# Turning an expert's activations behind the first chunk of the next expert's product, and the turned gating columns in another bank

## What is computed

```python
# second layer: 8 experts, each token is sent to 2 of them
for e in range(E):
    h = jax.nn.gelu(xf @ we1[e] + be1[e], approximate=False)   # 512 -> 1024
    y = h @ we2[e] + be2[e]                                    # 1024 -> 512
    out = out + combine[:, e:e + 1] * y
# fourth layer, from a zero state, so that only three of the four gates count
gates = xt @ Wi + b
c = sigmoid(i_) * tanh(g_)
h = sigmoid(o_) * tanh(c);  y = h @ Wo + bo
```

## Time and profile before

| | us |
|---|---|
| three timed runs, median (lowest to highest) | 488.34 (482.66 to 490.34) |
| the profiled execution, its own time | 483.48 |
| its span, from the first to the last instruction | 481.7 |
| TensorE busy | 439.2 (91% of the span) |
| VectorE busy | 396.8 (82%) |
| ScalarE busy | 281.5 (58%) |
| feed-forward experts, steps 0 to 7 | from about 59 to 164 |
| LSTM experts, steps 0 to 7 | from about 329 to 436 |

### The profile page before, as it was taken

One profiled execution on the slowest core, in us unless ns is written; L12 is line 12 of the kernel. 1 busy time (PEld: TensorE's weight loads), 2 busy tenths in 40 slices (PEclk: granted clock), 3 DMA queues, 4 the chain that ended last, 5 costly groups with the idle time before them and its releaser, 6 DMA issues.

```text
span 481.7 us, 6148 instructions
## 1 busy us (share of the span) xinstructions
PE 439.2 (91%) x2214; PEld 351.2 (73%) x2214; DVE 396.8 (82%) x645; ACT 281.5 (58%) x306; POOL 106.6 (22%) x128
## 2 busy tenths in 40 slices
PE   3988799999999976899999998979899899999895
PEld 1655578788888766587899996647678788887674
DVE  8989868898889854687999979785898998978764
ACT  2245468768876744143444446254988788858631
POOL 5641000111100050146787300030001211000300
PEclk9999999999999997799999999988999999999897
DMA  7931557899998838378677333235688999975801
GB/s 256 304 124 44 190 199 270 303 353 358 377 361 320 340 105 366 105 267 312 190 208 260 97 109 140 103 135 174 246 306 322 348 373 363 363 299 215 353 2 45
DMA packets 25780, 115.67 MB, mean 240 GB/s; under 512 B 7036, under 2 KB 7708, under 8 KB 14864
## 3 DMA queue, kind: packets, MB, share of 16 engines
q1 hardware_dynamic: 18400, 93.90, 52.7%
q0 software_dynamic: 7056, 21.26, 13.4%
q10 hardware_dynamic: 288, 0.03, 0.1%
HBM read 108.63 MB, written 6.55 MB: 239 GB/s over the span
## 4 chain that ended last, share of the span: by engine, by line
PE 63%; DVE 21%; ACT 6%; DMA 5%; issue 3%; POOL 1%; DVEq 1%; ACTq 0%; SPq 0%; POOLq 0%
PE bank L1506 11%; PE bank L1507 11%; PE bank L1511 11%; DVE wlo L928 7%; PE bank L1499 4%; PE bank L1882 3%; PE bank L1500 3%; PE bank L1884 3%; PE bank L1501 3%; PE bank L1520 2%; DMA y_tok<-y_rows,row_i 2%; PE bank L1771 2%; PE bank L1709 2%; DMA raw<-in_weights_dram 1%; ACT whi L673 1%
## 5 line engine op out<-in xcount | busy, mean ns | idle before, releaser
L928 DVE TENSOR_TENSOR wlo<-raw,whi 128x2048 fp32r<-128x2048 f32 x73 | 165.2, 2287 | 15.0 <-ACT whi L673 14.5
L673 ACT ACTIVATE whi<-raw 128x2048 fp32r<-128x2048 f32 x73 | 137.6, 1914 | 8.3 <-PE bank L1851 6.4
L1506 PE MATMUL bank<-whi,xe_hi 128*128 128x512 f32 x192 | 77.2, 402 | 2.8 <-ACT xe_hi L702 1.4
L1507 PE MATMUL bank<-wlo,xe_hi 128*128 128x512 f32 x192 | 75.9, 395 | 0.0
L1511 PE MATMUL bank<-whi,xe_lo 128*128 128x512 f32 x192 | 52.4, 394 | 0.0
L1506 PE MATMUL bank<-whi,hT_hi 128*128 128x512 f32 (+1 forms) x124 | 49.8, 405 | 2.1 <-ACT hT_hi L730 1.4
L615 POOL DMA_INDIRECT xg<-node_rows,idx x12 | 14.4, 1202 | 156.9 <-DVE idx L1191 156.9
L1507 PE MATMUL bank<-wlo,hT_hi 128*128 128x512 f32 (+1 forms) x124 | 48.1, 391 | 0.0
L648 POOL DMA_INDIRECT gath<-node_rows,src_i x34 | 41.6, 1224 | 15.2 <-DVE mp L1423 8.7
L1506 PEld LDWEIGHTS bank<-whi,xe_hi 128*128 128x128 f32 x192 | 36.1, 188 | 11.6 <-issue 2.2
L1511 PEld LDWEIGHTS bank<-whi,xe_lo 128*128 128x128 f32 x192 | 36.1, 188 | 8.6
(11 more groups left out here) (307 smaller groups left out, 854.2 us busy)
## 6 DMA issues: line engine op xcount, KB each, us to landing
raw<-in_weights_dram SPq DMA_DIRECT2D x85, 1024.0 KB, 6.3
y_rows<-y_sb POOLq DMA_DIRECT2D x16, 256.0 KB, 5.9
ea<-in_ea_dram SPq DMA_DIRECT2D x8, 256.0 KB
node_rows<-xn POOLq DMA_DIRECT2D x4, 256.0 KB, 2.5
gath<-node_rows,src_i POOLq DMA_INDIRECT x34
x<-in_x_dram SPq DMA_DIRECT2D x1, 512.0 KB, 3.8
gw<-in_L_ffn_gw_dram SPq DMA_DIRECT2D x1, 512.0 KB, 10.2
node_rows<-A_sb POOLq DMA_DIRECT2D x2, 256.0 KB, 4.4
```

The costliest lines, as they stand in the source:

```text
L673: act.activation(whi[n % SPL][:, :, :], raw[n % RAW][:, :, :], ACT.Copy).then_inc(hi_cut, 1)
L928: dve.tensor_tensor(wlo[n % SPL][:, :, :], raw[n % RAW][:, :, :], whi[n % SPL][:, :, :].bitcast(f32), ALU.subtract).then_inc(lo_cut, 1)
L1506: pe.matmul(ps, xh[:, blocks + k, :], whi[w % SPL][:, k, cs], start=first and k == 0, stop=False)
L1507: pe.matmul(ps, xh[:, blocks + k, :], wlo[w % SPL][:, k, cs], start=False, stop=False)
```

## The change

On TensorE `turn_h(e - 1)` moves from the end of step e - 1 into `first_product(e)`, behind its first chunk. That first chunk now waits for only the first of the two counts of `h_ok` (`2e - 1`), since the bank that it writes has been read by then. Only the last expert's activations are turned at the end of a step, as before. The gating columns of `turn_g` go to bank 0 instead of bank 5, so `turn_g` no longer waits for `hT_lo`, nor `turn_h` for `idx_ok`; `turn_g` waits for the `idx` before its own. `biases`, which writes bank 0 later, waits for the last `idx`. The runs for experts with more than 128 tokens keep their order. On ScalarE and VectorE the cuts of a step move ahead of `turned`.

```diff
@@ ScalarE, experts
                     if step >= 2:
                         outputs(step - 2)
+                    if step >= 2:
+                        cuts(run.last_out(step - 2) + SPL + 1)
                     if step >= 1:
                         turned(step - 1)
...
-                    if step >= 2:
-                        cuts(run.last_out(step - 2) + SPL + 1)
                     results(step)
@@ VectorE, slots and experts
-                        dve.tensor_scalar(idx[:, e:e + 1], B[5][:, at:at + 1], -1.0, 0.0, ALU.add, ALU.max)\
+                        dve.tensor_scalar(idx[:, e:e + 1], B[0][:, at:at + 1], -1.0, 0.0, ALU.add, ALU.max)\
...
+                    if step >= 2:
+                        cuts(run.last_out(step - 2) + SPL + 1)
                     if step >= 1:
                         turned(step - 1)
-                    if step >= 2:
-                        cuts(run.last_out(step - 2) + SPL + 1)
                     results(step)
@@ TensorE, biases
+                pe.wait_ge(idx_ok, (E - 1) * nth - 1)
@@ TensorE, turn_g
-                    if e >= 3:
+                    if 2 < e <= E:
                         pe.wait_ge(*run.slot_read(e - 1))
-                    if e >= 3:
-                        pe.wait_ge(run.hT_lo, run.banks_h * (e - 2 if e < E else e - 1))
+                    if e >= E:
+                        pe.wait_ge(run.hT_lo, run.banks_h * (e - 1))
...
-                        ins = pe.matmul(B[5][:, at:at + TURN], columns(e, n), turner[:, n, :],
+                        ins = pe.matmul(B[0 if e < E else 5][:, at:at + TURN], columns(e, n), turner[:, n, :],
@@ TensorE, first_product
                         if e >= 1 and c == 0:
-                            pe.wait_ge(run.h_ok, 2 * e)
+                            pe.wait_ge(run.h_ok, 2 * e - 1 if e < E else 2 * e)
...
+                        if 0 < e < E and c == 0:
+                            turn_h(e - 1)
@@ TensorE, turn_h and the end of a step
-                def turn_h(e, gathered):
+                def turn_h(e):
                     pe.wait_ge(run.h_ok, 2 * (e + 1))
-                    pe.wait_ge(*run.slot_read(gathered - 1))
+                    if e >= E:
+                        pe.wait_ge(*run.slot_read(e))
...
                     if step == E - 1:
                         with pe.If(number > 0):
                             pe.wait_ge(*run.slot_read(E))
-                    turn_h(step, min(step + 3, E))
+                        turn_h(step)
```

More of the change, by code:

```diff
@@ L1807, in job @@
                         gather_one(e + 1)
-                        turn_h(e, e + 1)
+                        turn_h(e)
                         if e > E:
```

## The result

The changed kernel took **494.06 us** (median of 4 executions, 490.12 to 496.55), the kernel before 487.76 us in the same comparison (482.66 to 490.34). The ratio is **1.0145, 95% interval 1.0088 to 1.0202**: slower by 1.5%, more than the scatter and less than 2%. The forecast of 487 us, +0.7 us, was wrong, and the time lies above the range of 481 to 492.

A forecast was written before the change was run, and what follows sets the result against it. TensorE, busy 439 of 482 us, bounds the kernel except where VectorE or ScalarE leads. Feed-forward +2.0 and LSTM -1.3 make +0.7: 484.2 on the profiled execution, 489.0 on the median; predicted 487, range 481 to 492.

The forecast's parts named there:

- the feed-forward layer: Feed-forward loop: expert 2 starts 0.38 us earlier, transposes cost 0.79 three times around experts 3 and 7; sum +1.99 us.
- the start of the LSTM layer: LSTM steps 0 to 4: turned copy 0.76 us later, yet expert 4 starts at 380.3 instead of 382.35.
- the gather for expert 5: LSTM layer: gather lands in time at its 6.2 us median, so the layer's gain of 1.3 us stays.
- Issued 0.76 later, with the median it lands at 389.1: LSTM expert 5's gather, issued 0.76 us later and taking the median 6.2 us, is in time.
- Moving `turned` behind the cuts costs nothing here: Feed-forward steps 3 to 6, VectorE: over 3.5 us of other TensorE work covers the later copies; cost nothing.
- The upper bound of +0.2 us: LSTM layer's worst case: expert 5's gather takes 8.8 us, lands at 391.7, and TensorE is 0.2 us later than before.
- The rival of the late gather: LSTM expert 5's gather late at 8.8 us: no LSTM gain, +2.2 us in all, 485.7; chance 0.12.
- The rival of the falling clock: Idle 1.9 us ahead of feed-forward expert 3 drops the clock to 1.2 GHz: +4.1 us, 487.6; chance 0.10.
- the turned copy: Rival: behind two cuts `hT_lo` misses the second product, 12 steps at some 0.5 us, +6; chance 0.07. Forecast counted nothing.

The follow-up runs named there:

- e12: Changed kernel, VectorE's row numbers ahead of its token copy, feed-forward transposes moved only for experts 3, 4 and 5; 484.21 us against 486.76, ratio 0.9944.
- e4: Changed kernel, but VectorE computes the row numbers ahead of its copy of the tokens, so the gather starts earlier; 489.95 us, ratio 1.0068 to the kernel before.
- e9: Kernel before with gating columns in bank 0 and, in the LSTM layer, only VectorE's cuts moved ahead of its turned copy; 490.46 us, ratio 1.0079.
- e1: Change in the feed-forward layer only, LSTM layer in the old order with gating columns in bank 0; 487.58 us against 488.0 before, ratio 1.0002.
- e3: Changed kernel, but VectorE copies the turned activations ahead of its cuts again, in both layers; 495.06 us, ratio 1.0191 to the kernel before.
- e2: Change in the LSTM layer only, feed-forward layer in the old order with gating columns in bank 0; 491.04 us, ratio 1.0058 to the kernel before.
- e7: e4's kernel with VectorE's small work moved behind the cuts for the next expert; 492.44 us, ratio 1.0147 to the kernel before.
- e5: Kernel before with only the gating columns' bank and its waits changed, old order in both layers; 487.18 us against 487.21, ratio 0.9962.
- e11: Kernel before with one edit, VectorE's row numbers ahead of its copy of the tokens; 486.34 us against 487.43, ratio 0.9977.
- e8: Kernel before with two VectorE edits, row numbers ahead of the token copy and small work behind the cuts; 486.13 us, ratio 0.994.
- e6: Change in the LSTM layer only, with VectorE's row numbers ahead of its token copy in both layers; 486.84 us, ratio 1.0001 to the kernel before.
- e10: Kernel before with the LSTM change, VectorE's row numbers first in both layers, feed-forward small work behind the cuts; 485.02 us, ratio 0.9959.

## Why the prediction was wrong, step by step

**Right: the feed-forward layer.** Forecast +1.99 us, +2.04 in the pair of profiles. The steps hold too: expert 2 came 0.39 earlier against the loop's start (0.38 forecast), the wait ahead of expert 3 was 1.57 (1.5 to 2) and ahead of expert 7 1.13 (over 1), and the transposes stand behind it at full price (98.81, eight in a row). Between them the delay stayed where it was forecast, at 1.20: against the loop's start the tokens of expert 4 came 1.16 later (102.69 and 101.62) and the first chunk of expert 7 1.18. e12 shows that the moved sets between them are free. The size has one reserve: the old order took 103.3 to 103.9 us in five other profiles, less than the 104.29 of before, so 2 to 3 us is what the profiles bear out, and that the forecast was met to 0.05 us is luck.

**Right: the start of the LSTM layer.** -2.05 forecast up to expert 4, -1.83 measured. `hT_hi` of expert 0 came 0.66 later against the last bias matmul of its step (345.58 and 341.67, against 341.42 and 338.17 in the earlier trace rows; 0.76 forecast, though its own sum of 342.15 less 341.42 makes 0.73, and its chunk of 3.03 stands in it as 3.09), there was no wait at the transposes, and a wait of 0.50 at the first chunk of expert 2 had moved behind `xe_hi`. With the gather free (e4) the layer gains 0.94 us, where 1.3 was forecast.

**Wrong: the gather for expert 5.** "Issued 0.76 later, with the median it lands at 389.1" failed. The issue came 0.97 later against the layer's start, as forecast or nearly so; but I took the median of twelve gathers though the trace showed one for this very gather, and held even the worst case to be the 8.8 us of the order before. Both came from reading `xg`'s landing as scatter of the DMA. For the most part it was a position: the instruction of the earlier trace rows took 3.49 of the 8.8 us on GpSimd, where its neighbour took 0.97, and the cut beside it ended 0.85 us before it. GpSimd's timeline shows it, and I had not read it. The other half of the failed step is "Moving `turned` behind the cuts costs nothing here". It weighed only the copy that moves back, and nothing was counted for what the cuts that move forward meet: their order on VectorE decides whether one cut or two stand in the gather's way (5.69 us instead of 3.49, landing in 11.5 instead of 8.8; e9 shows it by itself). The upper bound of +0.2 us was wrong by the length of a cut, and by what follows.

The landing at 11.5 us cost 3.88 us of waiting; the rest of the stretch's +4.88 is there without it too (10.05 us from expert 4 to the tokens in e4, against 9.15 before), of which the forecast had 0.71. The rival of the late gather had the right place and the right page, but its price, +0.2, was taken from the row of before, so it stayed at 485.7. The Trainium skill's page "GPSIMD Engine Reference", section "1. Specifications", was the one to follow: the one case of twelve that I counted for it was an instruction 2.5 us too long. The Trainium skill's page "SBUF — State Buffer", section "🔬 SBUF: two separate sides", says more: the shared pair of ports is locked for a whole instruction, the other engine fully blocked, and an instruction with two SBUF inputs takes it against a GpSimd instruction that reads SBUF. The traces agree with the blocking, since the gather's duration steps by whole cuts (0.97, 3.49, 5.69). The same section says that the pair goes to whichever of the two starts first; there the traces don't agree as they stand, for nine gathers that started 0.26 to 0.37 us ahead of a cut ended behind it. I had not weighed this page. That the ports are what the two engines share here is the page's word; the runs show that the cuts hold the gather up, and not by what.

**Wrong: the clock, at another place.** The rival of the falling clock expected it ahead of expert 3, where 1.57 us of idle time passed at full clock, as did 1.94 in e1 and 2.87 in e3 (2.13 ahead of expert 7 in e3 did not). It came behind the late gather instead, for 2.6 us. In the LSTM layer it followed each of the four waits of 3.0 us and more (at the tokens, in the changed kernel, e2, e7 and e9), for 6.8 us in the first (from 1.2 us before the wait's end) and 3.4 in the others, and never a gather in time. Behind the wait of 1.94 us of the earlier trace rows, which six profiles have, it came in e1, e5, e9 and e11, and stayed away in the kernel before and e8. So the row that I used against this rival, a pause of 1.94 us at full clock, was one outcome of two. Where it came, expert 1 to expert 2 took 14.50 to 14.52 us instead of 13.25, so the old LSTM order pays 1.25 us there in some executions, and the change, which has no such wait, was spared it; that the wait brings the low stretch about isn't tested alone. (That expert 0 to expert 1 took 13.5 to 13.6 us in e1, e5 and e9, and 11.92 before, is another thing: there the clock was still low from before the loop.) In the feed-forward layer e7's wait of 1.45 us was followed by a low stretch too. No run tells what decides.

**Right: the turned copy.** In the changed kernel it cost nothing behind the cuts that the traces show; ahead of them (e3) the feed-forward layer loses 9 us.

**What the step explains, and what stays open.** With the gather for expert 5 in time (e4) the ratio falls from 1.0145 to 1.0068. So the gather and the clock behind it are about half of the loss in time, 3.8 of 7.1 us, though they are 7 us in the pair of profiles. The 3.3 us that remain (1.4 to 5.3) are more than the 0.7 forecast. The 2 to 3 us of the feed-forward layer, less the 0.94 of the LSTM layer, would leave 1 to 2; whether there is more isn't clear of the noise.

## What to carry to other kernels

Read the duration of one DMA instruction on GpSimd, not only the median to landing: one that is 2.5 or 4.7 us longer than its neighbours stood behind VectorE here, and an edit that joined two of VectorE's long instructions nearly doubled that price. Issue such a gather a microsecond before a run of two-input instructions: none with a lead of 0.40 us or more was slow in these profiles. And price a step moved on one engine also for the engine that shares something with it, even where every semaphore says it is free.

## What the runs showed of the hardware

- In the fourteen profiles there are 168 of these gathers. 153 took 0.94 to 1.10 us on GpSimd, 15 took 2.77 to 5.69, and each of the 15 ended 0.84 or 0.85 us after the end of a cut. Four started ahead of two cuts without a pause and passed behind the second (the changed kernel, e2, e7 and e9). Where 0.1 us or more lay between the cuts (417.33 in the changed kernel, 394.78 in e12), and twice where the gather had started inside the first of two cuts without a pause (e3), it passed behind the first.
- All 15 started between 0.37 us before and 0.36 us after the start of a cut. All six that started inside a cut were slow. None that started 0.40 us or more before one was. In between both occur: 0.20 us ahead of a cut took 0.97 (394.94 in the kernel before), 0.26 ahead took 0.97 in e6 and e10, 3.37 in e12 and 5.57 in e7, 0.37 ahead took 0.98 at one place in e3 and 3.49 in the kernel before. What decides there stays open.
- From the end of the instruction to the landing the gather for expert 5 took 5.8 us in the changed kernel, 5.3 before, 4.2 in e4 and 6.1 in e11. That part scatters also where no cut was in the way (4.2 and 6.1); that the instruction's own time follows the cuts is all that is shown.
